# A fused Mamba, FP4, attention and QLoRA program on one core: its tail spread over two chunk times, with more work on TensorE and no loop

## The reference

```python
xn = _layernorm(x)
s = _L0_attn_ref(xn, ...)          # LN, Mamba block (D_INNER 512, 16 states, conv of 4 taps), residual, LN, FFN 256-1024-256 with gelu, residual
g = _silu(_L0_ffn_ref(xn, ...))    # FP4 (blocks of 16) gate/up 256-704, silu*up, quantized again, down 704-256
x = x + s * g
xn = _layernorm(x)
s = _L1_attn_ref(xn, ...)          # attention over the 2 rows of the "sequence" axis, 16 heads of 16
g = _silu(_L1_ffn_ref(xn, ...))    # three blocks: linear, LN, gelu, linear, + h (QLoRA weights)
x = x + s * g
# inside the Mamba block
def step(h, inp):
    dt_t, B_t, C_t, x_t = inp
    dA = jnp.exp(dt_t[..., None] * A)
    h = dA * h + dt_t[..., None] * B_t[:, None, :] * x_t[..., None]
    y = jnp.sum(h * C_t[:, None, :], axis=-1)
    return (h, y)
```

## Time and profile before

| | us |
|---|---|
| median of 3 executions | 2985.43 (2978.42 to 2988.90) |
| profiled execution, its own time | 2981.44 |
| its span, first to last instruction | 2979.3 |

### The profile page before, as it was taken

The page is one execution under the profiler, slowest core; times in us unless marked ns, Lnnn a source line. Parts: engine busy times, 40 slices in busy tenths (PEclk is TensorE's granted clock), DMA queues, the critical chain, the costliest instruction groups (busy, mean ns, idle before and its releaser), DMA issues.

```text
span 2979.3 us, 28883 instructions
## 1 busy us (share of the span) xinstructions
PE 1925.2 (65%) x7760; PEld 1465.3 (49%) x7760; DVE 1937.7 (65%) x2306; ACT 1486.6 (50%) x2992; POOL 1526.0 (51%) x1329
## 2 busy tenths in 40 slices
PE   0555857577685757667575776857667575765766
PEld 0333646455464545546454554645455464544644
DVE  2367767766676776667677666766666676766642
ACT  0255646446463544646464474645547364654532
POOL 1167555656355565536556463655556364555431
PEclk9956878778787878877787787878778786877877
DMA  5000000000000000000000000000000000000000
GB/s 143 4 11 1 1 1 11 1 12 1 11 1 0 12 1 11 1 12 1 1 11 1 12 1 11 1 0 12 0 11 1 12 1 0 11 1 8 1 8 4
DMA packets 31524, 25.55 MB, mean 9 GB/s; under 512 B 12038, under 2 KB 30278, under 8 KB 31318
## 3 DMA queue, kind: packets, MB, share of 16 engines
q1 hardware_dynamic: 31318, 23.23, 2.8%
...
## 4 chain that ended last, share of the span: by engine, by line
PE 23%; POOL 21%; issue 19%; ACT 19%; DVE 12%; POOLq 1%; ACTq 1%; DVEq 0%; DMA 0%
PE bank L488 9%; POOL drive L905 5%; ACT decay L723 4%; ACT L723 4%; PE bank L481 3%; DVE drive L1030 3%; PE bank L647 3%; POOL xd L1003 3%; PE bank L519 2%; POOL t_sm L929 2%; POOL wide L1008 2%; DVE dt L1221 2%; PE bank L603 2%; PE bank L537 1%; POOL drive L904 1%
## 5 line engine op out<-in xcount | busy, mean ns | idle before, releaser
L1030 DVE TENSOR_TENSOR_SCAN drive<-decay,drive 128x1032 f32<-128x1032 f32 x256 | 606.0, 2367 | 278.4 <-POOL drive L905 259.7
L905 POOL TENSOR_TENSOR drive<-wx,bc_sb 128x1024 f32<-128x1024 f32 x256 | 614.7, 2401 | 0.0
L904 POOL TENSOR_TENSOR drive<-carry,zero 128x8 f32<-128x8 f32 x256 | 124.9, 488 | 862.0 <-ACT carry L732 784.8
L655 PE MATMUL y_ps<-ident,decay 128*128 128x128 f32 x2048 | 353.8, 330 | 285.1 <-DVE decay L1035 279.3
L655 PEld LDWEIGHTS y_ps<-ident,decay 128*128 128x128 f32 x2048 | 307.6, 174 | 340.7 <-DVE decay L1035 292.8
L723 ACT ACTIVATE decay<-dt,aneg 128x256 f32<-128x256 f32 x1024 | 435.3, 499 | 1.5
L1035 DVE TENSOR_TENSOR decay<-drive,bc_ps 128x1024 f32<-128x1024 f32 x256 | 312.5, 1221 | 8.8
L664 PE MATMUL bc_ps<-bc,pick 64*128 64x256 f32 x512 | 157.2, 395 | 159.2 <-DVE decay L1035 159.1
L488 PE MATMUL bank<-w_l,op_b 128*128 128x256 f32 x384 | 177.2, 642 | 77.3 <-ACT op_b L813 45.7
L664 PEld LDWEIGHTS bc_ps<-bc,pick 64*128 64x128 f32 x512 | 96.9, 236 | 218.2 <-DVE decay L1035 167.4
L927 POOL TENSOR_TENSOR t_sm<-t_mv,epsc 128x2 f32<-128x2 f32 x80 | 49.3, 617 | 269.9 <-DVE t_mv L1046 269.9
...
## 6 DMA issues: line engine op xcount, KB each, us to landing
...
```

Source lines behind the costliest of these rows:

```text
L655: last = t.matmul(y_ps[j][:, g * P:(g + 1) * P], src(g, j), ident[:, :], start=(first and g == 0), stop=stop, is_transpose=True, skip_grou ...
L904: g_.tensor_tensor(d[:, :, 0], carry[:, n, :], zero8[:, :], ALU.add).then_inc(S["drive_ready"], 1)
L905: g_.tensor_tensor(d[:, :, 1:SEG].rearrange("p (g b) t -> p g b t", b=B), wx[par][:, :, :].rearrange("p g (b t) -> p g b t", b=B), bc_sb[n ...
L1030: v.tensor_tensor_scan(drv[:, :, :].rearrange("p s t -> p (s t)"), dec[:, :, :].rearrange("p s t -> p (s t)"), drv[:, :, :].rearrange("p s ...
```

## The change

Six things are changed together.

1. **Three chunks in flight.** The tail is cut into A (op to f2), B (xn1T to b1a) and C (b1T to b2b and the final sum). A and B of chunk c-1 and C of chunk c-2 run during the scan of chunk c; one more period without a scan stands at the end. `x1` and `h` have two buffers.
2. **FP4 moved forward.** All of the FP4 branch of chunk c (also `hqT` and `dn`) now runs in the first eleven slots of chunk c's own scan.
3. **Biases by TensorE.** b_f2, b_ao, the qkv biases and the six block biases are added by one more matmul into the same bank: 8 (or 2) rows of biases, 512 (or 384) wide.
4. **Conv and y by TensorE.** The four taps are folded into the weights (`w_tap`), and a `xi` bank now takes 16 fp32 matmuls, not 4. D * xc is a matmul by a diagonal (`skip_y`), and `sum_y` is two fp32 matmuls, 512 wide, by the identity in the place of eight transposes; y stands with channels on partitions, so that the transposes `ygT` go.
5. **Norms.** GpSimd keeps one operation (pow); VectorE adds eps and applies the norm, from PSUM for b0, b1 and b2.
6. **No loop.** All periods are written out, and all waits are on constants.

The core of the diff:

```diff
-NBANK = 3
-SPREAD = [n % 3 for n in range(NS - 1)] + [1]
+PE_SLOT = {
+    1: [("C", "b1T"), ("A", "op")],
+    2: [("M", "xqT"), ("C", "b1b")],
+    3: [("M", "g00"), ("M", "g01"), ("M", "u00"), ("M", "u01"), ("A", "u2T"), ("C", "h2T")],
+    4: [("M", "g10"), ("M", "g11"), ("M", "u10"), ("M", "u11"), ("A", "f10"), ("A", "f11"), ("C", "b2a")],
+    5: [("A", "f12"), ("A", "f13"), ("F", "uT")],
+    6: [("A", "f2"), ("C", "b2T"), ("F", "xi0")],
+    7: [("C", "b2b"), ("F", "xi1")],
+    8: [("F", "z0"), ("F", "z1")],
+    9: [("B", "xn1T"), ("F", "xp")],
+    10: [("B", "b0a"), ("B", "qkv0"), ("B", "qkv1"), ("B", "qkv2"), ("B", "qkv3"),
+         ("M", "hqT0"), ("M", "hqT1"), ("M", "hqT2")],
+    11: [("M", "dn"), ("F", "dt0"), ("F", "dt1")],
+    12: [("B", "b0T")],
+    13: [("B", "b0b")],
+    14: [("B", "ctxT"), ("B", "h1T")],
+    15: [("B", "ao"), ("B", "b1a")],
+}
-        PE_SLOT = {1: ["ygT0", "ygT1"], 2: ["op"], 4: ["u2T", "hqT0", "hqT1", "hqT2", "f10", "f11"],
-                   5: ["f12", "f13", "dn"], 6: ["f2"], 8: ["xn1T", "b0a"],
-                   9: ["qkv0", "qkv1", "qkv2", "qkv3"], 10: ["b0T"], 11: ["b0b"],
-                   12: ["ctxT", "h1T", "b1a", "ao"], 13: ["b1T", "b1b"], 14: ["h2T", "b2a"], 15: ["b2T", "b2b"]}
-        PE_SLOT_F = {2: ["uT"], 3: ["xi0", "xi1", "z0", "z1"], 6: ["xp"], 7: ["dt0", "dt1"]}
-        PE_SLOT_M = {13: ["xqT"], 14: ["g00", "g01", "u00", "u01"], 15: ["g10", "g11", "u10", "u11"]}
...
+                if row is not None:
+                    last = t.matmul(dst[:, 0:B * D], ident[0:NROW, row:row + 1].to_broadcast([NROW, P]),
+                                    b_rows[:, None, :].to_broadcast([NROW, B, D]), start=False, stop=True,
+                                    skip_group_check=True)
...
+                    for a in range(2):
+                        for tap in range(NTAP):
+                            for k in range(KD):
+                                last = t.matmul(dst[:, a * TOK:(a + 1) * TOK],
+                                                w_tap[:, tap, k, (2 * m + a) * P:(2 * m + a + 1) * P],
+                                                u_t[:, k, :, tap:tap + TC],
...
+            def sum_y(hc, stop):
+
+                for m in range(2):
+                    last = t.matmul(y_ps[m][:, :], ident[:, :], hc[:, 4 * m:4 * m + 4, 1:SEG],
+                                    start=False, stop=stop, skip_group_check=True)
+                last.then_inc(S["y_summed"], 1)
...
+            def norm_apply(dst, src, name, chunk, done):
+
+                dve.wait_ge(S[name], value(chunk, name, 1))
+                for j in range(B):
+                    last = v.tensor_scalar(dst[:, j, :], src[:, j, :], t_mv[:, j, 0:1], rstd[:, j:j + 1],
+                                           ALU.subtract, ALU.mult)
+                last.then_inc(S[done], 1)
...
-            with eng.Fori(1, NC - 2, 2) as c:
+                for c in PERIODS:
+                    pe_body(pe, c)
```

1134 lines of the change are left out of this document (535 added, 599 removed).

## The result

| | before | after |
|---|---|---|
| median | 2986.2 us (4 runs, 2978.4 to 2988.9) | 2952.7 us (4 runs, 2944.5 to 2958.7) |
| ratio | 1 | 0.9893, 95% interval 0.9877 to 0.9909 |
| profiled span | 2979.3 us | 2956.9 us |
| granted clock, mean | 0.782 | 0.865 |

The change made the kernel 1.1% faster. 2841 had been forecast (4.9% faster), with a range that holds the result.

What follows compares the result with a forecast made beforehand. Waits, not one full engine, bound the kernel; after, TensorE's 114.9 us plus a 44 us chain give 159, with hand-overs 3 and clock 3 165 a period. With set-up and ends the span is 2835, the median 2841 us; range 2755 to 2990.

Steps and rivals of the forecast that it cites:

- No loop: Writing out the loop over periods: costed at nothing, ends 0 and 1 us per two periods.
- The chain behind dt1: From dt1's fill through softplus, attention, states 13 to 15 and b1a to yg: 44 us a period in all.
- all hand-overs: Some 30 hand-overs on a period's path at 0.1 each: +3 us.
- TensorE's stretch: From yg to dt1's fill, slots 1 to 11: TensorE without a gap but for banks, 114.9 us.
- The clock term: TensorE's restarts before slots 15 and 1 at 1.2 GHz: 3 us each, half taken, +3 a period.
- The ends: Outside the full periods: set-up 126, first front 54, period 0 118, period 1 155, period 15 132, end 105 us.
- the wrong case: Slots 2 to 10: clock under 0.92, TensorE idle over 5 us, or ScalarE full between table loads, would show the forecast wrong.
- signs of right: Period 160 to 170; PE busy near 150 without gaps in slots 1 to 11, clock at 0.95 or more there.
- the third (0.14): Rival, chance 0.14: missed waits, three banks served by two engines, cost 8 us more a period, 173, giving 2950.
- the b-matmuls behind gelu: In the missed-waits rival: two b-matmuls waiting for gelu behind a table load, named as where to look; no size of their own.
- the forecast case: Chance 0.57: TensorE sets slots 1 to 11, softplus and b1a's chain the rest; period 160 to 170, 2770 to 2910.
- The clock rival: Chance 0.17, slower: bank gaps and weak bias rows keep TensorE's clock low in slots 1 to 11; 0.88 gives about 3050.

Runs made afterwards that it cites:

- E10: The kernel before with its loop over two periods written out and nothing else changed: 2937.6 us, 170.7 a period against 174.1.
- E17: The kernel before with periods 1 and 2 written out and the other twelve in three passes of four periods: 2975.5 us, ratio 0.997.
- E5: The changed kernel with ScalarE's copy of state 11's carry ahead of state 13's broadcast copy and decay in slot 12: 2880.6 us, ratio 0.964.
- E7: The changed kernel with softplus's two tmp_u products on VectorE instead of GpSimd: 2906.2 us, ratio 0.971.
- E6: The changed kernel with ao and b1a moved from slot 15 to the end of slot 14 on TensorE: 2890.6 us, ratio 0.969.
- E9: The changed kernel with matmul products added in both TensorE waits of slot 10, six ahead of qkv1 and four ahead of qkv2: 2905.4 us, ratio 0.976.
- E4: The changed kernel with twelve matmul products added in TensorE's wait for b0T's gelu in slot 13: 2943.3 us, ratio 0.987.
- E15: The changed kernel with mended order (2698.3 us), plus matmul products added in TensorE's gaps of slots 13 and 1: 2682.4 us, ratio 0.898 against before.
- E1: The changed kernel without its twelve bias matmuls a period: 2792.9 us, ratio 0.937.
- E8: The changed kernel with VectorE's order in slots 10 and 11 changed to free the banks of x_proj and b0a sooner: 2888.7 us, ratio 0.967.

## Why the forecast was too low

**The loop.** "*No loop:* periods with the loop's branch in them are not longer than their neighbours ... I cost it at nothing." This step failed, in the kernel's favour: E10 shows 3.4 us a period, 44 us in all. The row was misread besides. The period of 173.4 is period 6, an even one, and has the branch in it (VectorE's 2.43 us at 1327.67); the odd ones without it take 173.8 to 175.0, so that the comparison, read rightly, would have had the branch make a period shorter. What hid it is the clock of slot 3 (E17). And no comparison of neighbours could see the register work, which stood in both. The sign was in section 4 of the profile's page: 19% issue. The Trainium skill (Runtime: NRT & Kernel Launch, Instruction fetch mechanics), which I cited, speaks of the branch: the rows agree, with 2.4 to 2.7 us on VectorE each time. E17 shows long periods without one.

With this the measured gain is accounted for, if the loop would have cost after what it cost before (after was not run in a loop), and the rest is the surprise: before with the loop written out has 170.7 a period, after 170.9. Deeper tail, conv, biases and norms together gave nothing, where the forecast had them at 174.1 - 165 = 9.

**The chain behind dt1.** "Together 44, and with 114.9 the period is 159 at the high clock." This step failed against the kernel. From dt1's fill (1284.06) to the next yg (1333.4) it is 49.3 us, and 48.65 in an odd period, where the sum had 44 less the 1.4 of yg itself, 42.6. By its items: softplus 7.1 (6.8). State 13's decay 3.2 (3.4). Then 2.95 for carry copy and drive, which I had left out (E5). Scan and multiply 4.3 (3.6). Attention and b0b 8.6 (5.8), two of its operations waiting for GpSimd (E7). dt and wx 3.7 (5.8). States 14, 15 and quant_scale 10.3 (8.8), one operation of 2.14. To yg 9.2 (8.4), 3.9 of it for b1a (E6). The 3 us that stood for all hand-overs were half of what was missing.

**TensorE's stretch.** 114.9 from yg to dt1 (the eleven slots add up to 110.8, not 110.6); measured 118.25 (odd) and 122.3 (even). The prices of y sum (1.81 from start to start), conv (7.1 for 16) and transposes were right. The biases were not: 1.05 and 0.84 for 0.90 and 0.68. The bank wait of 3.3 us for x_proj's split was in the sum (2.9 measured), but it was costed as itself; what it brought was the low clock behind it, 3.7 us a period by E9.

**The clock term.** The 3 us were for the restarts ahead of slots 15 and 1. Those rows are at the low clock (3.55 to 3.75 for D * xc, 1.9 at the high), but by E4 and E15 they are hardly on the path. The Trainium skill (TensorE: Matmul & The Clock Gate, Part 4: PE-mode transpose) would have had the restarts warmer without the sum's transposes; this trace does not show it, they begin at 1.2 GHz with the new sum as with the old. Nor does its rule hold in the set-up of before, where TensorE does nothing but transposes from 98.5 us on and the same twelve go from 2.37 to 1.67 us as the clock rises:

```profile
103.17 2.37 PE L326 MATMUL bank<-ident,down_raw 128*128 128x128 f32 x12
105.56 1.67 PE L326 MATMUL bank<-ident,qkv_raw 128*128 128x128 f32 x12
```

**The ends.** Up to the first yg +18.6: the set-up 8 of it (132.2 + 1.2 for 125.4 to its last fold), all clock, which E1, with the same set-up, doesn't have; the first front 48 for 54; period 0 134.6 for 118, because dt1 is now filled 93 us after its start and the 41 behind it have no other work beside them, where it was 48 before. Periods 1 and 15 +6 and +11 from the same chain. The end +10, clock by E15. With 13 x 5.9 = 76 that is the 122 between 2835 and 2956.9.

**What would show it.** VectorE's waits for b1b and b2b went, its waits in slots 8, 12 and 13 came, as said. The scan of state 14 stands 29.8 us after dt1 (25). From the end of yg to dt1 TensorE is idle for 4.0 and 4.4 us, under the 5 of the wrong case, and the clock is 0.92 and 0.95, between the signs of right (0.95) and wrong (under 0.92); up to the first gap of slot 10 it is 0.98 and 0.97.

**The rivals.** What came is the third (0.14): waits that I missed eat the gain, 170.9 for its 173, 2953 for its 2950. Its first half was right in place and mechanism, "three banks served in one order by two engines" (E8); the second, the b-matmuls behind gelu, was not on the path (E4). That the forecast case had 0.57 rested on a sum whose last third was written with free engines. The clock rival (0.17) decided at 0.92 and the even periods touch it: its "small gaps for banks" are what dropped the clock (E9, 3.7 a period), while no run shows that the bias rows did.

**The side** was right by luck, for a reason that had been costed at nothing. Against the kernel before with its loop written out, after is 0.4% slower (ratio 0.989, 0.988 to 0.991, against 0.985, 0.983 to 0.987). What the deeper tail is worth alone was not tried; that 14 of its 18 us of waits went is shown, and that as much came back by the biases (9.3), the conv (3.6) and the new waits (E5 to E8, 15) too.
